# Expert visits as two half tiles of 64 rows: rows stationary, weights moving

## The chip, the cores and the metric

One Trainium2 chip, one core. The metric is the device time in microseconds (us) of one execution; smaller is better. The kernel is written by hand: every engine has its own instruction list, and semaphores order them.

## What is computed

Patch embedding of 32 images (1,184 tokens of 256 numbers), one block of linear attention with a gate and a norm, then a mixture of experts. All data is float32. The part that the change touches, cut from the reference:

```python
logits = x @ gate_weight.T                       # 32 experts in 4 groups
...                                              # 2 groups of 4, then 6 experts per token
tw = tw / (tw.sum(-1, keepdims=True) + 1e-20) * ROUTED_SCALE
eo = silu(x @ w_gate[e]) * (x @ w_up[e]) @ w_down[e]      # 256 -> 128 -> 256
routed = sum over the 6 experts of tw * eo
shared = silu(x @ shared_w_gate) * (x @ shared_w_up) @ shared_w_down
lg = topidx[:, 0] // 2                           # one of 16 anchor experts, 256 -> 64 -> 256
out = routed + shared + 0.1 * anchor(lg)
```

## The kernel before, in words

**Front part.** Blocks of two token tiles (111 tokens each) go through embedding, attention, norm and routing as a hand-written pipeline. When a block is routed, GpSimd (POOL) scatters each token's row (256 numbers and its weights and destinations, `ROW` = 322 words) with an indirect DMA into `rows_d` in DRAM, once for each of its 7 choices: 77 scatters in all (`scatter`). There is one list of rows for each of the 48 experts (32 routed, 16 anchors).

**Visit table.** After the last block is routed, VectorE (DVE) works out a table from the lengths of the lists: for each visit the place of the expert's weights in `W`, the first row, the column of the weight and the place of the sum tile (some 85 small instructions, ending in `cols_ok`). TensorE (PE) turns it into one row (`table_rows`), DVE copies it to `table`, and a second PE product with two DVE steps makes the mask `valid` (`slot_bounds`). The weights of all experts are in SBUF (`W`) by then. While the table is made PE does matmuls that serve nothing (`stay_busy`).

**Visits.** There are `XT` = 112 visits of 128 rows: 25 of anchors, 87 of routed experts. A visit `i` is, in order: SyncE (SP) reads its first row from the table with a register load and issues one DMA of 128 rows into `G` (six buffers, `load_rows`); PE transposes it in two pieces (`turn_rows`, L812); ScalarE (ACT) or DVE copies the transpose to SBUF (`turned_copy`, L985, L1580) and ACT copies the expert's gate and up weights from their place in `W`, which is known only at run time, to a fixed buffer `UPW` (`copy_up`, L981); PE multiplies, weights stationary and rows moving, 4 products of 128x128x128 for a routed expert and 2 for an anchor (`up`, L823); ACT takes silu (L990), DVE multiplies by the up half (`hidden`, L1597); PE multiplies with the down weights, 256 columns (`down`, L838). A float32 product is two PE instructions. PE does up(i), the transposes of i+2, down(i-1), up(i+1).

**Results.** A routed visit on a full tile of one list ("F") is weighted by ACT and sent. A visit on a tile in which rows of two lists meet ("M", "X", and the anchors) is weighted and added by DVE into a tile of sums (`accumulate`, L1589), which is sent when its last visit is in. POOL sends with an indirect DMA of 128 rows into `sums_d` (L483), 66 in all. The tiles of sums lie in `spent` and `ring`, which POOL fills with zeros first (L476, L480).

**End.** When all is sent, SP loads the seven parts of each token back from `sums_d` (L419), DVE adds them to `h`, and SP writes the output.

Of the kernel before, what the change touches and what calls it, by code (L numbers as in the profile page):

```python
# [17 lines left out]
F32 = mybir.dt.float32  # L18
I32 = mybir.dt.int32
# [42 lines left out]
DUMMY_ROW = P + LISTS * LIST_ROWS  # L62
# [7 lines left out]
ROWS_PACKED = -(-TOKENS * TOPK // P)  # L70
LAST_FILLED = TOKENS * TOPK % P
FULL = -(-(TOKENS * TOPK - EXPERTS * (P - 1)) // P)
MIXED = ROWS_PACKED - FULL
EXTRAS = EXPERTS - 1
ANCHOR_PACKED = -(-TOKENS // P)
ANCHOR_TILES = ANCHOR_PACKED + ANCHORS - 1
KINDS = "A" * ANCHOR_TILES + "FFX" * 12 + "XM" * 6 + "XMM" * 13
XT = len(KINDS)
INDEX = [KINDS[:i].count(k) for i, k in enumerate(KINDS)]
TILE_AXIS, EXTRA_AXIS = 1000, 2000  # L80
RING = D + 1
GB = 6
PL = 3 * EXPERTS + ANCHORS


def routed(i):
    return KINDS[i] != "A"


def summed(i):  # L90

    return KINDS[i] != "F"


def sums_before(i):
    return sum(summed(k) for k in range(i))


def copied_by_act(i):
    return KINDS[i] != "F"  # L100


def copies_before(i):
    return sum(copied_by_act(k) == copied_by_act(i) for k in range(i))


def number_of(i):

    return {"A": 0, "F": TILE_AXIS, "M": TILE_AXIS + FULL, "X": EXTRA_AXIS}[KINDS[i]] + INDEX[i]


FIRST_ROUTED = ANCHOR_TILES
EARLY_COLS = 19482
TRI4 = 3 * LISTS
SMALL = TRI4 + 23
PIECES = [[(0, 4), (4, 8), (8, NT)]] * (CHOICES - 1) + [[(0, 4), (4, 7), (7, 9), (9, 10), (10, NT)]]
assert KINDS.count("F") == FULL and KINDS.count("M") == MIXED and KINDS.count("X") == EXTRAS
assert all(KINDS[:i].count("X") >= min(EXTRAS, INDEX[i] + 1) for i in range(XT) if KINDS[i] == "M")
assert FULL * D <= ANCHOR_COLS and XT <= P
# [4 lines left out]
def build(nc, pt, wt, posr, brow, wqkv, wo, wg1, wg2, lnwb, gwt, gbias, sgu, sd, wx,  # L124
          ident_c, cmask_c, turn_c, parity_c, cs_c, before_c, small_c, out):
    with ExitStack() as ctx:
# [56 lines left out]
        def dense(*shape):  # L183
# [5 lines left out]
            if len(shape) == 2:  # L189
# [16 lines left out]
        mixed = spent[:, 0:MIXED * RING]  # L206
        mixed_rows = mixed.bitcast(I32)
# [5 lines left out]
        of_lists = small[:, 0:3 * LISTS].rearrange("p (q l) -> p q l", q=3)  # L213
        iota_a, base0, tri4 = small[:, LISTS:LISTS + ANCHORS], small[:, 2 * LISTS:3 * LISTS], small[:, TRI4:TRI4 + 16]
        pcol, number, of_number, tile_number, spare_row, last_tile, first_w = (small[:, TRI4 + 16 + q:TRI4 + 17 + q]
                                                                                  for q in range(7))
        ring = sb("ring", [P, ANCHOR_PACKED * RING])
        h = sb("h", [P, NT, D])
        ring_rows = ring[:, :].bitcast(I32)
        token_row = sb("token_row", [P, 2, NT], I32)  # L220
        to_rows = sb("to_rows", [P, NT])
        spare = sb("spare", [P, 2])
# [32 lines left out]
        whole = sb("whole", [P, 2 * LISTS], I32)  # L255
        tcol = sb("tcol", [P, 24])
        valid = turn
# [3 lines left out]
        def later(n):  # L261
# [6 lines left out]
        GT = later(2 * D).rearrange("p (u k s) -> p u k s", u=2, k=KC)  # L268
        S = later(2 * P).rearrange("p (u s) -> p u s", u=2)
        H = later(2 * P).rearrange("p (u s) -> p u s", u=2)  # L270
        tabs = e_sb[:, 0:at[0]]
        edges = later(2 * P).rearrange("p (u s) -> p u s", u=2)
        H_anchor = edges
        UPW = sb("UPW", [P, 2, UP_COLS])
        wcol = sb("wcol", [P, XT])
        tok_full = sb("tok_full", [P, FULL], I32)
        Y = W[:, 0:FULL * D].rearrange("p (f d) -> p f d", d=D)
        parts = W[0:TP, 0:CHOICES * NT * D].rearrange("p (c t d) -> p c t d", c=CHOICES, t=NT)

        B = [ctx.enter_context(nc.psum_tensor(f"B{i}", [P, 512], F32)) for i in range(8)]  # L280

        rows_d = nc.dram_tensor("rows_d", [DUMMY_ROW + 2 * P, ROW], F32).ap()
        sums_d = nc.dram_tensor("sums_d", [SPARE_ROW + P, D], F32).ap()
# [22 lines left out]
        g_ld = [sem(f"g_ld{u}") for u in range(GB)]  # L306
        edges_ok, valid_ok, mixed_zero = sem("edges_ok"), sem("valid_ok"), sem("mixed_zero")
        gt_by = {True: sem("gt_by_act"), False: sem("gt_by_dve")}
        T_ps, U_ps, silu_ok, H_ok, upw_ok, D_ps, Y_ok = (
            sem("T_ps"), sem("U_ps"), sem("silu_ok"), sem("H_ok"), sem("upw_ok"), sem("D_ps"), sem("Y_ok"))  # L310
        meta_ok, acc_ok, ring_ok, ids_ok, spared = sem("meta_ok"), sem("acc_ok"), sem("ring_ok"), sem("ids_ok"), sem("spared")
        sent_anchor, sent_full, sent_mixed = sem("sent_anchor"), sem("sent_full"), sem("sent_mixed")
# [4 lines left out]
        def entry(engine, q, i, top):  # L317

            return nc.values_load(table[0:1, q, bass.ds(i, 1)], engines=(engine,), min_val=0, max_val=top,  # L319
                                  skip_runtime_bounds_check_because="the table is computed within these bounds")  # L320
# [28 lines left out]
        def _(sp):  # L349
# [26 lines left out]
            of_list = rows_d[0:LISTS * LIST_ROWS, :].rearrange("(l r) n -> r l n", r=LIST_ROWS)  # L376
            for half in range(2):
                sp.dma_start(of_list[half * P:(half + 1) * P, :, :],
                             padrow[:, :].unsqueeze(1).to_broadcast([P, LISTS, ROW])).then_inc(empty, 16)
            sp.dma_start(W[:, 0:late[0]], wx[:, 0:late[0]]).then_inc(ld["lists"], 16)  # L380

            for half in range(2):
                sp.dma_start(rows_d[DUMMY_ROW + half * P:DUMMY_ROW + (half + 1) * P, :], padrow[:, :]).then_inc(ini_d, 16)
# [17 lines left out]
            sp.wait_ge(ini_d, 16 * 4)  # L401
# [3 lines left out]
            def load_rows(i):  # L405
                if i == FIRST_ROUTED:
                    sp.wait_ge(scat, 16 * NT * TOPK)
                if i >= GB:

                    sp.wait_ge(T_ps, i - GB + 1)  # L410
                    sp.wait_ge(meta_ok, i - GB + 1)
                row = entry(mybir.EngineType.SP, 1, i, DUMMY_ROW + P)
                sp.dma_start(G[:, i % GB, :], rows_d[bass.ds(row, P), :]).then_inc(g_ld[i % GB], 16)
# [6 lines left out]

            for i in range(XT):
                load_rows(i)
                if i == XT - 16:
                    sp.wait_ge(sent_anchor, 16 * ANCHOR_PACKED)
                    sp.wait_ge(sent_full, 16 * FULL)
                    load_part(TOPK)
            sp.wait_ge(D_ps, XT)
            sp.wait_ge(sent_mixed, 16 * MIXED)
# [9 lines left out]
        def _(pool):  # L438
# [10 lines left out]
            pool.memset(ring[:, :], 0.0).then_inc(ring_ok, 1)  # L449
# [25 lines left out]
            pool.wait_ge(hs_ok, NB)  # L475
            pool.memset(spent[:, 0:until_scattered], 0.0).then_inc(mixed_zero, 1)  # L476
            pool.wait_ge(scat_anchor, 16 * NT)
            pool.wait_ge(scat, 16 * NT * TOPK)
            pool.wait_ge(ini_d, 16 * 4)
            pool.memset(spent[:, until_scattered:MIXED * RING], 0.0).then_inc(mixed_zero, 1)  # L480

            def send(rows, src, done):
                pool.indirect_dma_start(sums_d, bass.IndirectOffsetOnAxis(ap=rows, axis=0), src, None).then_inc(done, 16)  # L483

# [1231 lines left out]
```

## Time and profile before

| what | value |
|---|---|
| device time, median of 3 runs | 418.36 us (414.25 to 418.94) |
| profiled execution, span | 412.1 us |
| PE busy | 343.3 us (83%) |
| PE weight load busy | 299.1 us (73%) |
| DVE busy | 278.0 us (67%) |
| ACT busy | 190.0 us (46%) |
| POOL busy | 181.7 us (44%) |
| visit stage, from the first transposes to the first load of parts | 203.1 to 379.95 us |

The span is the time from the first to the last instruction of one profiled execution; a device time of its own is not given for that execution, and the median of the runs is 6.3 us above the span. "Busy" is the time in which an engine had an instruction at work. Times below count from the start of the span.

### The profile page before, as it was taken

The numbers are of one execution on the slowest core, as the hardware profiler recorded it, in microseconds if no ns is written. First come the engines' busy times: TensorE is split into PE (matmuls) and PEld (weight loads), VectorE is DVE, ScalarE is ACT, GpSimd is POOL, SyncE is SP. The second block draws the span as 40 slices with busy tenths as digits, with TensorE's granted clock in tenths as the row PEclk, the third lists the DMA queues.
The fourth block names the chain that finished last, engine by engine and source line by source line (L and its number), as shares of the span: only waits on it lengthen the run. The fifth ranks groups of instructions, "written<-read, shape, count | busy, mean of one in ns | idle before, by whom it ended". The sixth has DMA issues, their size and how long they took to land.

```text
span 412.1 us, 8817 instructions
## 1 busy us (share of the span) xinstructions
PE 343.3 (83%) x2552; PEld 299.1 (73%) x2552; DVE 278.0 (67%) x1171; ACT 190.0 (46%) x471; POOL 181.7 (44%) x159
## 2 busy tenths in 40 slices
PE   5999999999899968773889999999999999994000
PEld 3786978779687857561677789999999999993000
DVE  0466789989798886798357775555565665666675
ACT  1152153441545233400157777777877777771000
POOL 6000000588888768767871374344422344433000
PEclk9999999999999997985989999999999999998555
DMA  7999999986698643694555576555555559531998
GB/s 234 298 335 335 329 341 328 420 320 119 123 337 252 126 96 86 218 387 137 152 162 130 167 214 180 162 158 165 165 145 162 166 155 291 168 113 58 303 303 245
DMA packets 55823, 88.44 MB, mean 215 GB/s; under 512 B 16145, under 2 KB 46521, under 8 KB 55513
## 3 DMA queue, kind: packets, MB, share of 16 engines
q1 hardware_dynamic: 38192, 67.66, 52.9%
q0 software_dynamic: 16720, 19.48, 17.8%
q10 hardware_dynamic: 864, 0.73, 0.6%
q8 instruction: 21, 0.34, 0.3%
q14 instruction: 26, 0.21, 0.2%
HBM read 50.62 MB, written 37.09 MB: 213 GB/s over the span
## 4 chain that ended last, share of the span: by engine, by line
PE 60%; DVE 20%; DMA 8%; issue 3%; ACT 3%; SPq 3%; DVEq 2%; POOLq 0%
PE B L823 20%; PE B L838 10%; PE B L514 6%; PE B L812 5%; DMA W<-sums_d 4%; PE B L549 4%; PE B L632 3%; PE B L598 2%; PE B L618 2%; DVEq L319 2%; DMA e_sb<-rows_d 2%; SPq L419 2%; DVE ring L1589 1%; PE B L656 1%; DMA W<-in_pt 1%
## 5 line engine op out<-in xcount | busy, mean ns | idle before, releaser
L457 POOL DMA_INDIRECT rows_d<-spent,slot x77 | 104.1, 1352 | 97.3 <-issue 90.9
L823 PEld LDWEIGHTS B<-e_sb,UPW 128*128 128x128 f32 x796 | 105.4, 193 | 10.7 <-issue 5.5
L823 PE MATMUL B<-e_sb,UPW 128*128 128x128 f32 x796 | 108.9, 278 | 1.5 <-issue 1.5
L1597 DVE TENSOR_TENSOR e_sb<-e_sb,B 128x128 f32<-128x128 f32 (+1 forms) x112 | 32.3, 288 | 62.2 <-ACT e_sb L990 55.8
L981 ACT COPY UPW<-W 128x512 f32 (+1 forms) x112 | 63.9, 570 | 22.2 <-issue 13.9
L838 PE MATMUL B<-W,e_sb 128*128 x224 | 69.3, 391 | 0.8 <-DVE e_sb L1597 0.8
L483 POOL DMA_INDIRECT sums_d<-spent x32 | 31.1, 972 | 48.7 <-DVE spent L1589 47.9
L812 PE MATMUL B<-ident,e_sb 128*128 128x128 f32 x224 | 43.1, 274 | 1.9 <-DMA e_sb<-rows_d 1.8
L990 ACT ACTIVATE e_sb<-B 128x128 f32<-128x128 f32 (+1 forms) x112 | 30.9, 276 | 22.2 <-PE B L823 20.8
L514 PE MATMUL B<-W 128*111 128x256 f32 (+1 forms) x132 | 34.2, 406 | 4.6 <-DMA W<-in_pt 4.5
L483 POOL DMA_INDIRECT sums_d<-W,tok_full x24 | 23.2, 966 | 30.3 <-ACT W L995 29.7
L838 PEld LDWEIGHTS B<-W,e_sb 128*128 128x128 f32 x224 | 34.0, 192 | 3.5 <-issue 1.7
L985 ACT COPY e_sb<-B 128x256 f32<-128x256 f32 x88 | 32.3, 367 | 4.6 <-PE B L812 4.6
L514 PEld LDWEIGHTS B<-W 128*111 128x111 f32 (+1 forms) x132 | 23.3, 184 | 12.2 <-DMA W<-in_pt 5.3
L1589 DVE SCALAR_TENSOR_TENSOR spent<-B,wcol,spent 128x256 f32<-128x256 f32 (+1 forms) x63 | 30.4, 482 | 1.7 <-DVE spent L1574 0.8
L812 PEld LDWEIGHTS B<-ident,e_sb 128*128 128x128 f32 x224 | 28.5, 144 | 2.3 <-DMA e_sb<-rows_d 2.1
L1626 DVE TENSOR_TENSOR h<-h,W 112x1024 f32<-112x1024 f32 (+3 forms) x23 | 23.2, 1047 | 8.4 <-DMA W<-sums_d 8.4
L1289 DVE TENSOR_TENSOR e_sb<-B,spent 111x444 f32<-111x444 f32 (+1 forms) x44 | 23.6, 597 | 4.1 <-PE B L598 4.1
L1566 DVE TENSOR_TENSOR wcol<-e_sb,turn 128x1 f32<-128x1 f32 x112 | 17.2, 153 | 4.0 <-PE B L812 3.8
L598 PE MATMUL B<-W 32*111 32x222 f32 (+1 forms) x176 | 15.5, 369 | 4.8 <-ACT W L909 4.8
L549 PE MATMUL B<-W 128*128 128x222 f32 (+1 forms) x96 | 18.1, 341 | 0.6 <-ACT W L886 0.6
L606 PE MATMUL B<-spent 128*128 128x256 f32 x70 | 18.6, 414 | 0.0
(250 smaller groups left out, 524.0 us busy)
## 6 DMA issues: line engine op xcount, KB each, us to landing
e_sb<-rows_d SPq DMA_DIRECT2D x112, 161.0 KB, 2.3
rows_d<-spent SPq DMA_DIRECT2D x2, 7728.0 KB, 44.4
W<-in_wx SPq DMA_DIRECT2D x1, 6643.0 KB
W<-sums_d SPq DMA_DIRECT2D x13, 448.0 KB, 9.4
W<-in_wx SPq DMA_DIRECT2D x10, 516.5 KB, 9.5
W<-in_wx SPq DMA_DIRECT2D x1, 4576.0 KB, 18.7
W<-in_pt SPq DMA_DIRECT2D x4, 666.0 KB, 6.9
W<-sums_d SPq DMA_DIRECT2D x7, 336.0 KB, 11.1
```

The source lines that it names most:

```text
L457: pool.indirect_dma_start(rows_d, bass.IndirectOffsetOnAxis(ap=slot[0:n, t, j:j + 1], axis=0), xrow[0:n, t, :], None).then_inc(done, 16)
L483: pool.indirect_dma_start(sums_d, bass.IndirectOffsetOnAxis(ap=rows, axis=0), src, None).then_inc(done, 16)
L514: m = pe.matmul(B[0][0:TILES[t], i * D:(i + 1) * D], patch_view(b)[:, c, at:at + TILES[t]], w_patch[:, c, :], start=c == 0, stop=c == PC - 1)
L549: m = pe.matmul(B[4 + half][:, c * BT:c * BT + n], w_qkv[:, k, lo:lo + P], xnT[:, k, 0:n], start=k == 0, stop=k == KC - 1)
L812: m = pe.transpose(B[i % 2][:, k * P:(k + 1) * P], G[:, i % GB, k * P:(k + 1) * P], ident[:, :])
L823: mm = pe.matmul(B[2 + i % 2][:, m * P:(m + 1) * P], UPW[:, i % 2, at:at + P], GT[:, i % 2, k, :], start=k == 0, stop=k == KC - 1)
L838: pe.matmul(B[6 + i % 2][:, 0:D], hid[:, i % 2, :], weights, start=True, stop=True).then_inc(D_ps, 1)
L981: act.copy(UPW[:, i % 2, 0:n], W[:, bass.ds(e, size)][:, 0:n]).then_inc(upw_ok, 1)
L985: act.copy(GT[:, i % 2, :, :].rearrange("p k s -> p (k s)"), B[i % 2][:, 0:D]).then_inc(gt_by[True], 1)
L990: act.activation(S[0:n, i % 2, :], B[2 + i % 2][0:n, 0:P], ACT.Silu).then_inc(silu_ok, 1)
L1589: dve.scalar_tensor_tensor(sums, B[6 + i % 2][:, 0:D], wcol[:, i:i + 1], sums, ALU.mult, ALU.add).then_inc(acc_ok, 1)
L1597: dve.tensor_tensor(out[0:n, i % 2, :], S[0:n, i % 2, :], ups, ALU.mult).then_inc(H_ok, 1)
```

## The change

The visits get another shape. A visit still has 128 row slots, but as two halves of 64 rows, each from any list: 17 visits of anchors, 71 routed, 88 in all (`VISITS`), taken two at a time in 44 rounds (`ROUNDS`). A list's last half may hold fewer than 64 rows of its own; the slots left over are sent to spare rows of `sums_d`. Every row is in one visit only, so nothing is added up: each visit is sent by itself, 88 sends.

In a round PE transposes four pieces (as before), multiplies with the rows stationary (64 columns of the array for each half, `tile_position=(0, lo)`) and the weights moving (256 columns for routed, 128 for anchors), then goes to the down products of the round before, the transposes of two rounds on, and two transposes of the hidden rows, which the new layout needs. The first half's weights are read where they lie in `W`; the second half's are copied by DVE to `up_w` and `down_w`. DVE picks the row's weight and destination with a comparison (`columns`), and multiplies by the weight in `hidden`. ACT copies the results of both visits at once. SP reads four first rows and issues four DMAs of 64 rows a round, with buffers for three rounds. The table has fewer steps; the lists' area is filled with zeros for 64 rows a list and no longer 256.

```diff
@@ SP
-                row = entry(mybir.EngineType.SP, 1, i, DUMMY_ROW + P)
-                sp.dma_start(G[:, i % GB, :], rows_d[bass.ds(row, P), :]).then_inc(g_ld[i % GB], 16)
+                if r >= GB // 2:
+                    sp.wait_ge(T_ps, r - GB // 2 + 1)
+                    sp.wait_ge(meta_ok, r - GB // 2 + 1)
+                rows = [entries(mybir.EngineType.SP, 2 + half, r, LAST_ROW - HALF) for half in range(2)]
+                for j in range(2):
+                    for half in range(2):
+                        sp.dma_start(G[half * HALF:(half + 1) * HALF, (2 * r + j) % GB, :],
+                                     rows_d[bass.ds(rows[half][j], HALF), :]).then_inc(g_ld[r % (GB // 2)], 16)
@@ POOL
-            pool.memset(spent[:, 0:until_scattered], 0.0).then_inc(mixed_zero, 1)
...
+            for v in range(VISITS):
+                if v % 2 == 0:
+                    pool.wait_ge(Y_ok, v // 2 + 1)
+                    pool.wait_ge(meta_ok, v // 2 + 1)
...
+                pool.indirect_dma_start(sums_d, bass.IndirectOffsetOnAxis(ap=row_to[:, v:v + 1], axis=0), results(v),
+                                        None).then_inc(done, 16)
@@ PE
-            stay_busy(12, 3, w_sgu)
+            stay_busy(7, 3, w_sgu)
             table_rows()
+            spread_columns()
             shared_down(3)
-            slot_bounds()
@@
+            def up(r, own_weights):
+                pe.wait_ge(GT_ok, r + 1)
+                pe.wait_ge(up_staged, r + 1)
+                for j in range(2):
...
+                    for k in range(KC):
+                        for half, w in enumerate((first, second)):
+                            lo = half * HALF
+                            m = pe.matmul(B[2 + r % 2][lo:lo + HALF, j * D:j * D + n], GT[:, r % 2, j, k, lo:lo + HALF],
+                                          w[:, k * n:(k + 1) * n], start=k == 0, stop=k == KC - 1, tile_position=(0, lo))
+                m.then_inc(U_ps, 1)
+            def turn_hidden(r):
+                pe.wait_ge(H_ok, r + 1)
...
+                for j in range(2):
+                    m = pe.transpose(B[4 + r % 2][:, j * P:(j + 1) * P], H[:, j, :], ident[:, :])
+                m.then_inc(HT_ps, 1)
+            def down(r, own_weights):
...
+                    for half, w in enumerate((first, second)):
+                        lo = half * HALF
+                        m = pe.matmul(B[6 + r % 2][lo:lo + HALF, j * D:(j + 1) * D], HT[:, j, lo:lo + HALF], w,
+                                      start=True, stop=True, tile_position=(0, lo))
...
+                up(r, own_weights)
+                if r >= 1:
+                    down(r - 1, before_own)
+                if r + 2 < ROUNDS:
+                    turn_rows(r + 2)
+                turn_hidden(r)
@@ ACT
+            for r in range(ROUNDS):
+                hidden_silu(r)
+                if r >= 1:
+                    result_copy(r - 1)
+                hidden_copy(r)
+                if r + 2 < ROUNDS:
+                    turned_copy(r + 2)
@@ DVE
+            def stage_up(r):
+                places = weights_of(mybir.EngineType.DVE, 1, r)
...
+                if r >= 2:
+                    dve.wait_ge(U_ps, r - 1)
+                for j in range(2):
+                    hidden, size = widths(2 * r + j)
+                    n = KC * 2 * hidden
+                    m = dve.tensor_copy(up_w[:, (2 * r + j) % 4, 0:n], W[:, bass.ds(places[j], size)][:, 0:n])
+                m.then_inc(up_staged, 1)
+            def stage_down(r, places):
...
+                    m = dve.tensor_copy(down_w[:, (2 * r + j) % 4, :], W[:, bass.ds(places[j], size)][:, n:n + D])
+                m.then_inc(down_staged, 1)
+            def columns(r):
+                dve.wait_ge(T_ps, r + 1)
...
+                    m = dve.scalar_tensor_tensor(own[:, j, :, :], iota_to.unsqueeze(1).to_broadcast([P, 2, TO_ROW]),
+                                                 expert_col[:, v:v + 1], both, ALU.is_equal, ALU.mult)
+                step(m)
+                dve.reduce_sum(wcol[:, r % 2 * 2:r % 2 * 2 + 2], own[:, :, 0, :], axis=AX.X).then_inc(weight_ok, 1)
+                step(dve.reduce_sum(to_sum[:, :], own[:, :, 1, :], axis=AX.X))
+                dve.tensor_tensor(row_to[:, 2 * r:2 * r + 2], to_sum[:, :], spare_to[:, 2 * r:2 * r + 2], ALU.add).then_inc(meta_ok, 1)
...
+            for r in range(ROUNDS):
+                hidden(r)
+                if r + 2 < ROUNDS:
+                    places.append(stage_up(r + 2))
+                if r + 1 < ROUNDS:
+                    stage_down(r + 1, places[r + 1])
+                    columns(r + 1)
```

## Rows read from the trace of the kernel before

**Rows 1.** Stretches of time: from:to, length, busy time of each engine, PE clock.

```profile
178.80:192.60 13.80, 5.49 (x23) 4.39 (x22) 12.81 (x85) 0.00 (x0) 11.05 (x9) 0.75 0.80 272
...
240.50:373.10 132.60, 132.60 (x1031) 128.20 (x1031) 77.39 (x346) 102.18 (x259) 54.42 (x58) 1.00 0.58 169
380.00:412.10 32.10, 0.00 (x0) 0.00 (x0) 19.96 (x20) 0.00 (x0) 0.00 (x0) 0.50 0.92 275
```

**Rows 2.** Timeline of one routed visit: start, length, engine, line, idle and releaser.

```profile
302.33 1.05 PE L823 MATMUL B<-e_sb,UPW 128*128 128x128 f32 x8
...
303.23 0.38 PE L812 MATMUL B<-ident,e_sb 128*128 128x128 f32 x2
...
303.43 0.28 ACT L990 ACTIVATE e_sb<-B 128x128 f32<-128x128 f32 x1 [0.27 <-PE B L823]
303.44 0.60 PE L838 MATMUL B<-W,e_sb 128*128 x2
...
303.73 0.29 DVE L1597 TENSOR_TENSOR e_sb<-e_sb,B 128x128 f32<-128x128 f32 x1 [0.56 <-ACT e_sb L990]
```

**Rows 3.** Timeline of PE, attention of tile 0: products in four column tiles.

```profile
36.45 0.98 PE L618 MATMUL B<-e_sb,W 111*32 111x111 f32 x32
37.35 0.60 PE L539 MATMUL B<-ident,W 111*128 111x111 f32 x4
37.88 0.98 PE L618 MATMUL B<-e_sb,W 111*32 111x111 f32 x32
```

**Rows 4.** Groups by form, routed stage: count, busy us, mean ns, idle before.

```profile
L981 ACT COPY UPW<-W 128x512 f32 x86 | 53.2, 618 | 15.9 <-issue 9.8
L985 ACT COPY e_sb<-B 128x256 f32<-128x256 f32 x63 | 23.1, 366 | 0.0
L1589 DVE SCALAR_TENSOR_TENSOR spent<-B,wcol,spent 128x256 f32 x30 | 14.5, 485 | 1.2 <-DVE spent L1574 0.8
```

**Rows 5.** Groups by form of DVE, whole span: wide operations from SBUF.

```profile
L1626 DVE TENSOR_TENSOR h<-h,W 112x512 f32<-112x512 f32 x1 | 0.7, 685 | 0.0
L1525 DVE TENSOR_SCALAR e_sb<-ident,tcol 128x128 f32<-128x128 f32 x1 | 0.3, 275 | 0.0
```

**Rows 6.** Timeline, 187.3 to 188.8 us: DVE beside a scatter of POOL.

```profile
187.38 1.35 POOL L457 DMA_INDIRECT rows_d<-spent,slot  x1 [0.30 <-issue]
187.38 0.24 DVE L1497 TENSOR_SCALAR e_sb<-e_sb,tcol 128x32 f32<-128x32 f32 x1
...
188.09 0.61 DVE L1501 COPY e_sb<-e_sb 128x16 f32<-128x16 f32 x1
```

**Rows 7.** SP's row loads (L413) and register loads (L319, by stretch): ns min/median/max.

```profile
L413 SPq DMA_DIRECT2D e_sb<-rows_d x112: 332/333/808, 196.8 to 363.4; - x112
...
DMA to landing us min/median/max: 2.2/2.3/6.2
...
L319 SPq TENSOR_LOAD <-scratch x8: 285/1160/1447, 195.3 to 206.6; - x8
...
L319 SPq TENSOR_LOAD <-scratch x102: 262/268/712, 212.5 to 363.0; - x102
```

**Rows 8.** POOL's last scatters and its routed sends: ns min/median/max.

```profile
L457 POOL DMA_INDIRECT rows_d<-spent,slot x19: 1348/1349/1354, 175.1 to 207.2; - x19
...
DMA to landing us min/median/max: 4.9/5.7/10.5
...
L483 POOL DMA_INDIRECT sums_d<-spent x30: 963/964/967, 301.8 to 372.8; - x30
```

**Rows 9.** Timeline: the table's first step, what waits for it, scatters landed, sends, end.

```profile
178.83 0.19 DVE L1441 SCALAR_TENSOR_TENSOR e_sb<-base,small 128x32 f32<-128x32 f32 x1
...
192.59 1.87 PE L711 MATMUL B<-ident,tcol 128*1 128x128 f32 x8 [8.31 <-DVE tcol L1524]
...
214.50 3.26 POOL L480 MEMSET spent<- 128x3791 f32 x1 [2.10 <-issue]
...
379.95 11.10 SPq L419 DMA_DIRECT2D W<-sums_d  x19
```

More of the change, by code:

```diff
@@ L1422, in tab @@
                 return v
-            starts, ends, total, of_tile, mine = tab(PL), tab(PL), tab(E), tab(E), tab(PL)
-            facts = tab(4 * PL).rearrange("p (q l) -> p q l", q=4)
-            offset, many, shifted, slot_tile = (facts[:, q, :] for q in range(4))
-            held, begin, end, full, lead, behind = tab(LISTS), tab(LISTS), tab(LISTS), tab(E), tab(LISTS), tab(LISTS)
-            new, away, some, rounded, over, span, own = (tab(LISTS), tab(LISTS), tab(LISTS), tab(E), tab(E), tab(ANCHORS),
-                                                         tab(LISTS))
@@ L1447, in _ @@
-            step(dve.tensor_copy(full, whole[:, 0:E]))
-            dve.scalar_tensor_tensor(held[:, LR], full, -float(P), total, ALU.mult, ALU.add)
-            step(dve.tensor_tensor_scan(ends[:, R], ones_of, full, float(TILE_AXIS), ALU.mult, ALU.add))
-            dve.tensor_copy(first_c, ends[:, E - 1:E])
-            dve.tensor_scalar(some, held, 0.0, None, ALU.is_gt)
-            dve.tensor_tensor(starts[:, R], ends[:, R], full, ALU.subtract)
-            step(dve.tensor_tensor_scan(end[:, LR], ones_of, held[:, LR], 0.0, ALU.mult, ALU.add))
@@ L1467, in _ @@
-            step(dve.tensor_copy(lead[:, 1:LISTS], whole[:, 0:LISTS - 1]))
-            dve.tensor_tensor(new[:, 1:LISTS], lead[:, 1:LISTS], lead[:, 0:LISTS - 1], ALU.is_equal)
-            dve.scalar_tensor_tensor(away, lead, -float(P), begin, ALU.mult, ALU.add)
-            dve.scalar_tensor_tensor(over, of_tile, -float(P), rounded, ALU.mult, ALU.add)
-            dve.tensor_tensor(span, span, lead[:, LA], ALU.subtract)
-            dve.tensor_scalar(starts[:, M], lead[:, LR], first_c, None, ALU.add)
@@ L1473, in _ @@
-            step(dve.tensor_scalar(ends[:, M], of_tile, first_c, None, ALU.add))
-            dve.scalar_tensor_tensor(own[:, LR], new[:, LR], -1.0, away[:, LR], ALU.add, ALU.mult)
-            dve.scalar_tensor_tensor(own[:, LA], new[:, LA], -1.0, away[:, LA], ALU.add, ALU.mult)
-            dve.scalar_tensor_tensor(over, over, 0.0, some[:, LR], ALU.is_gt, ALU.mult)
-            step(dve.tensor_tensor(span, span, some[:, LA], ALU.mult))
-            dve.tensor_tensor_scan(shifted[:, M], new[:, LR], own[:, LR], 0.0, ALU.mult, ALU.add)
```

567 lines of the change are left out of this document (230 added, 337 removed).

## The prediction

> **What bounds the kernel now.** I read the stretches first [rows 1]. From 240.5 to 373.1 us, the 86 routed visits between the first and the last up product, PE is busy for all 132.6 us at full clock; ACT (102.2), DVE (77.4) and POOL (54.4) are not. 132.6/86 gives 1.54 us a visit. One visit's timeline [rows 2] shows how PE fills it: 8 up instructions from 302.33 to 303.23, so 0.112 us each for 128 columns, two transposes at 0.11 (303.23 to 303.44), and two down instructions of 256 columns in 0.44 until the next up at 303.88. Ahead of it are the 25 anchor visits, and ahead of those the table: DVE works alone from 178.8 to 192.6 (85 instructions, PE clock 0.75) [rows 1], and PE's `table_rows` waits 8.3 us for it [rows 9]. Behind the visits the parts come back from 379.95 on, 32.1 us at 275 GB/s on which the change has no hand [rows 1, 9]. So the question is what a round costs, and when the routed rounds can begin.
>
> **PE's work in a round.** Transposes: 4 of rows and 2 of hidden rows, 6 x 0.11 = 0.66 us. Up: 8 products, 16 instructions of 256 columns at 0.22. Down: 4 products, 8 instructions at 0.22. One behind the other that is 3.46 + 1.73 us; in pairs, half. Whether column tiles run beside each other the trace does show: attention's L618 uses four tiles of 32 columns with a full depth of 111 rows and a different moving operand in each, and 32 instructions take 0.98 us with the last one's tail [rows 3]. At 111/128 x 0.112 = 0.097 each they would take 3.1 us alone; the last begins some 0.72 us in, so four ran at a time. I take pairs: 1.73 + 0.865. The change back to a full array is in the same rows: the last L618 ends at 37.43 and, with 0.26 us of its own length, began at about 37.16; L539 begins at 37.35, 0.09 us late against the step of 0.097. The other way L618 begins at 37.88 and L539's fourth at about 37.69, 0.09 late again. L539's three steps take 0.60 - 0.26 = 0.34 and not 0.29, 0.05 more. Two changes a round: 0.26. PE's round is 0.66 + 1.73 + 0.87 + 0.26 = 3.52 us for a routed pair, against 2 x 1.54 = 3.09 before: more for each visit, but 71 visits and not 87. 35.5 x 3.52 = 125 us against 87 x 1.54 = 134. An anchor round is 0.66 + 0.9 + 0.87 + 0.26 = 2.7 us.
>
> The Trainium skill, "TensorEngine Tiling (Array Packing)", Key Properties, says that changing the tiling mode drains TensorE, a rule that speaks against mixing full transposes and half tiles in each round. By the rows it costs 0.26 us a round, 11 us over 44 rounds; free of it the round would be 3.26 us.
>
> **Does PE get its data in time?** I lay one round out from the start of its up products (T = 0). Last up instruction begins at 1.5, and ends as modelled 0.38 later, ACT's silu follows 0.04 behind (303.43, [rows 2]): 1.93. Silu of 256 columns: 0.28 for 128 and 0.1 more, to 2.32. DVE's two products with the weight, 0.2 + 0.35 (0.485 for 256 columns from PSUM [rows 4]; 1.05 ns a column): 2.85. PE does down(r-1) and the row transposes until 3.2, so `turn_hidden` doesn't wait. ACT: silu 0.38, results 0.58, hidden rows 0.37, turned rows 0.58 (0.366 for 256 columns, 0.83 ns for each more, [rows 4]), 1.9 us in all; ACT is not the bound, and loses `copy_up`, 53.2 us.
> DVE then does what is new. A register load, 0.3. Two copies of 512 columns and two of 256, SBUF to SBUF. No such copy is in the trace. Above: an operation of two sources, 0.685 for 512 [rows 5]. Below: one source, 0.24 for 32 columns and 0.275 for 128 [rows 5, 6], 0.4 ns a column, so 0.45 for 512. I take the second, the nearer kind; in steps (without the tail of each) about 0.32 + 0.32 + 0.19 + 0.19, with addresses 1.2 us; by the first it would be 1.9. `columns` is five small operations with two waits, 0.9. DVE's round: 0.5 + 0.3 + 1.2 + 0.9 = 2.9 us (3.6 by the dear price), ending at T = 5.0.
> SP: two register loads (0.27 each in this stretch, [rows 7]; if each register needs its own, four), four DMAs at 0.333 + 0.2 for addresses and sequencing: 2.85 us, or 3.4. The last lands 2.3 us after its issue: 4.8 us from `meta_ok` to rows. The load of round r waits for `columns(r-3)`, done at T = 5.0 of slot r-4, and `turn_rows(r)` is at T = 2.75 of slot r-2: 2P + 2.75 >= 5.0 + 4.8, P >= 3.53 us. Before, this chain had six visits of room; now it is as long as PE's round, and everything that makes DVE later adds half of itself to P.
> What makes DVE later is POOL. At 188.09 a copy of 16 columns takes 0.61 us and ends with POOL's scatter that began at 187.38 (188.73); a like operation at the scatter's start, 187.38, takes 0.24 [rows 6]. A scatter holds such DVE operations in its second half. Before, the visits had none from SBUF to SBUF; now four a round meet two sends of 0.96 us [rows 8]. `result_copy` ends at T = 3.4, so the first send's second half (3.9 to 4.4) falls on the down copies: I take 0.4 us, P = (5.4 + 4.8 - 2.75)/2 = 3.73, and **3.75** as the forecast. POOL itself needs 2 x 1.3 = 2.6 us, under P: 88 sends and not 66 cost nothing while that holds.
>
> **The table.** About 27 operations with 10 waits take the place of 85: 0.2 + 0.3 + 0.35 + 0.35 + 0.4 + 0.6 + 0.65 + 0.35 for the dependent steps up to `cols_ok`, with a hold by POOL about 4 us, where 13.8 were. The table is ready some 10 us sooner. What is late next: SP's first rows, from about 187 us (the last anchor scatter has 17 behind it at 1.35 + 0.30, so it begins at 207.2 - 28 = 179, and lands 5.7 to 10.5 us after its issue, [rows 6, 8]). POOL still scatters until 208.6, and there SP's register loads take 1.16 us [rows 7]: 4.6 us a round. Rounds 0 to 4 are issued by 209.5, then one in 2.85. All scatters have landed at 214.5, when POOL's second fill starts [rows 9], so round 8, the first with routed rows, may be loaded. The chain of buffers puts `turn_rows(8)` at 224.5 and slot 8, the first routed one, at **227.5**, where before the first routed up product ran at 240.5. With quick anchor slots it would be 223; with four register loads 235. The fills with zeros before the visits and DVE's sums go, hidden already; the smaller zero fill of the lists frees writes in the front part, for which no engine but POOL waits, and POOL's last scatter is set by the last block's slots: nothing.
>
> **The end.** From the last slot's start: `turn_hidden` done at 3.1 + 0.3, copy 0.37, down 0.9 + 0.2, result 0.58, two sends 2.3, landing 1.5: 9.3 us, against 6.85 before (373.1 to 379.95).
>
> **Sum**, in the span of the profiled execution: 227.5 + 35 x 3.75 + 9.3 + 32.15 = 400.2 us, against 412.1. Gains: 13 us ahead of the routed rounds, 1.4 in them, less 2.5 at the end. The median of the runs lies 6.3 us above the span: **406.5 us**.
>
> **Rivals.**
> 1. *PE sets the round* (P = 3.52, quick anchor slots): the port hold misses DVE's copies. 223 + 123.2 + 9.3 + 32.15 + 6.3 = 394 us. For it: ACT, DVE and SP are each under 3 us. Against: the load chain is 3.53 without any delay.
> 2. *DVE is held for whole sends*, or its copies cost the dear price: columns end 1.2 us later (P >= 4.1), DVE's own round is 4.2 to 4.4. P = 4.3: 227.5 + 150.5 + 9.3 + 32.15 + 6.3 = 425.8, slower than before. It decides from P = (418.36 - 6.3 - 32.15 - 9.3 - 227.5)/35 = 4.09. The Trainium skill, "SBUF — State Buffer", Who interferes with whom, has this mechanism: a VectorE copy that uses both port pairs and a GpSimd operation lock each other out for the whole instruction. Rows 6 agree in kind, but the operation at the scatter's start ran free, so the hold is less than whole there.
> 3. *The half tiles don't overlap*: the sequence per product is pass, pass, other half, and fp32 with 64 columns is not in the trace. Then P = 3.46 + 1.73 + 0.66 + 0.26 = 6.1, anchor slots 4.4: 236 + 213.5 + 12 + 32.15 + 6.3 = 500 us. Against it, rows 3, made of the same two-pass products.
>
> **Chances.** Forecast (P 3.6 to 4.0, 401 to 415 us) 0.46; rival 1 0.2; rival 2 (415 to 436) 0.27; rival 3 0.07. A change of 2% is about what a measurement of this kernel tells from none: 410.0 and 426.7 us. Faster: 0.2 and 0.34 of the forecast's 0.46, 0.54. Within: 0.12 and 0.18 of rival 2, 0.30. Slower: 0.16. The range for 8 in 10: 392 (rival 1 with P 3.5) to 432 (P 4.3 with slot 8 at 234); rival 3 is left out.
>
> **What the profile after would show.** Right: up instructions of 256 columns beginning in pairs, about 1.75 us from the first up to the first down of a round; a period of 3.75 us; DVE's first copy 0.4 to 0.5 us, stage_down copies stretched beside a send; PE's idle time put down to the row DMAs or to DVE's columns; `table_rows` 10 us earlier; first routed up near 227.5. Wrong: PE steps of 0.22 with no pairs (rival 3); a period over 4.1 with DVE busy above 90% (rival 2); the tail longer than 32 us. My sum would also fail if PE's clock fell in the gaps of the anchor rounds and stayed low, which no row of the visits before shows.

## The result, and the profile after

The changed kernel takes 452.57 us (median of 4 runs, 451.65 to 455.45) beside 418.65 us of the kernel before (4 runs, 414.25 to 420.54): a ratio of 1.085, interval 1.078 to 1.092. It is slower, outside the range of the prediction. Medians here and below are of all executions, ratios and their 95% intervals of those in the faster of the two states in which a kernel runs.

Stretches of the kernel after, as in [rows 1]: from:to, length, busy time of PE, PEld, DVE, ACT and POOL, PE's granted clock, share and rate of the DMA engines.

```profile
181.30:185.70 4.40, 3.32 (x12) 2.40 (x10) 4.10 (x19) 0.00 (x0) 3.48 (x3) 0.83 1.04 386
...
211.30:245.80 34.50, 25.70 (x234) 19.15 (x234) 17.34 (x81) 12.58 (x30) 12.05 (x13) 0.82 0.44 127
245.80:403.50 157.70, 131.01 (x1046) 83.03 (x1046) 94.15 (x388) 64.12 (x142) 71.64 (x71) 0.97 0.47 140
414.60:450.40 35.80, 0.00 (x0) 0.00 (x0) 20.40 (x20) 0.00 (x0) 0.00 (x0) 0.50 0.94 247
```

The first row is the table, 4.4 us where [rows 1] have 13.8. The second is the eight anchor rounds, the third the routed ones from the first to the last up product: 157.7 us for 35 periods, 4.51 us each, with PE busy for 131.0 of them, where 35 x 3.52 = 123.2 were foreseen. Before, PE was busy for all of its 132.6 us. So the larger part of the loss in this stretch is not work of PE, but 27 us in which it stands. Who it stands for is in the page, part 5 (busy, mean ns, idle before, releaser):

```profile
L806 PE MATMUL B<-W,e_sb 128*64 x352 | 84.6, 388 | 5.7 <-issue 2.6
L806 PE MATMUL B<-up_w,e_sb 128*64 128x256 f32 (+1 forms) x352 | 84.8, 388 | 0.0
L790 PE MATMUL B<-ident,e_sb 128*128 128x128 f32 x176 | 30.8, 301 | 43.9 <-DMA e_sb<-rows_d 43.8
```

Over the whole kernel `turn_rows` (L790) waits 43.8 us for row DMAs. In the routed stretch alone it is 21.8 of the 27 us; 4.1 more are waits ahead of the up products (L806). The timeline of PE in a round that nothing disturbs:

```profile
336.32 0.42 PE L806 MATMUL B<-W,e_sb 128*64 x1
336.32 0.43 PE L806 MATMUL B<-up_w,e_sb 128*64 128x256 f32 x1
336.58 0.38 PE L806 MATMUL B<-W,e_sb 128*64 x1
336.59 0.38 PE L806 MATMUL B<-up_w,e_sb 128*64 128x256 f32 x1
...
338.09 0.38 PE L832 MATMUL B<-W,HT 128*64 x1
...
339.06 0.66 PE L790 MATMUL B<-ident,e_sb 128*128 128x128 f32 x4
339.55 0.38 PE L816 MATMUL B<-ident,H 128*128 128x128 f32 x2
340.19 0.42 PE L806 MATMUL B<-W,e_sb 128*64 x1 [0.25 <-DVE up_w L1478]
```

The two halves begin 0.01 us apart, then nothing for 0.21 us: full pairs. From the first up to the first down product it is 1.77 us (predicted: about 1.75), and from there to the transposes 0.97. The round is 3.87 us, and 3.87 is the least that any routed round shows; I had 3.52.

A disturbed round, as the chain of waits gives it piece by piece (start, length, what):

```profile
296.89 0.53 SPq L303
...
297.45 0.48 SPq L303
...
298.10 0.47 SPq L406
...
298.75 0.47 SPq L406
...
299.41 0.47 SPq L406
...
300.06 4.33 DMA e_sb<-rows_d
...
304.43 0.66 PE B L790 x4
305.09 0.22 PE B L816 x2
305.31 0.12 issue
305.43 3.50 PE B L806 x16
```

Two register loads of two values, 0.53 and 0.48 us ([rows 7] have 0.268 for one value); four issues of 64 rows at 0.47 and 0.18 between them ([rows 7]: 0.333 for 128 rows); then 4.33 us from the last issue until PE can use the rows (2.6 to 2.7 in most rounds where PE waits for them and they come quickly, 2.45 in one). PE has stood since 302.3, and when it goes on its up products take 3.50 us and not 1.77: over 305.4 to 308.9 the granted clock is 0.54, so nearly all of it at the lower of TensorE's two levels (1.2 and not 2.4 GHz), where 301.9 to 304.4, in which PE stood for 2.1 us, still showed 1.00. This late row cost twice.

The front, line by line of SP's queue (ns min/median/max), the loads of rounds 0 to 2 while GpSimd scatters:

```profile
L303 SPq TENSOR_LOAD <-scratch x6: 555/1133/2639, 190.2 to 207.0; - x6
...
L406 SPq DMA_DIRECT2D e_sb<-rows_d x12: 468/827/1812, 191.8 to 210.9; - x12
```

### The profile page after: what moved, and what is told of

It is laid out like the page before. It is cut to its first block, busy times and chain, and to the rows that moved or that the text cites. A ratio compares the mean times of both kernels' runs of the same rounds, so it can differ in the third digit from the quotient of the medians.

```text
span 450.4 us, 8512 instructions
## 1 busy us (share of the span) xinstructions
PE 335.6 (75%) x2622; PEld 246.9 (55%) x2622; DVE 281.3 (62%) x1141; ACT 142.9 (32%) x312; POOL 199.6 (44%) x178
## 4 chain that ended last, share of the span: by engine, by line
PE 27%; DVE 17%; issue 16%; DMA 14%; SPq 11%; POOL 10%; ACT 3%; DVEq 1%; POOLq 0%
POOL sums_d L474 10%; SPq L406 5%; DMA e_sb<-rows_d 5%; DMA W<-sums_d 5%; PE B L490 5%; PE B L806 4%; SPq L303 3%; PE B L525 3%; DMA rows_d<-spent,slot 2%; PE B L608 2%; PE B L574 2%; DMA W<-in_wg 2%; SPq L413 1%; PE B L594 1%; PE B L790 1%
## 5 line engine op out<-in xcount | busy, mean ns | idle before, releaser
L474 POOL DMA_INDIRECT sums_d<-spent,turn x56 | 57.6, 1029 | 72.6 <-ACT spent L1002 63.8
L806 PE MATMUL B<-W,e_sb 128*64 x352 | 84.6, 388 | 5.7 <-issue 2.6
L806 PE MATMUL B<-up_w,e_sb 128*64 128x256 f32 (+1 forms) x352 | 84.8, 388 | 0.0
L806 PEld LDWEIGHTS B<-W,e_sb 128*64 128x64 f32 x352 | 46.8, 147 | 31.4 <-issue 18.0
L790 PE MATMUL B<-ident,e_sb 128*128 128x128 f32 x176 | 30.8, 301 | 43.9 <-DMA e_sb<-rows_d 43.8
L790 PEld LDWEIGHTS B<-ident,e_sb 128*128 128x128 f32 x176 | 19.7, 148 | 62.2 <-DMA e_sb<-rows_d 46.7
L474 POOL DMA_INDIRECT sums_d<-W,turn x32 | 32.8, 1025 | 38.9 <-ACT W L1002 34.0
L832 PE MATMUL B<-W,HT 128*64 x176 | 46.5, 388 | 0.5 <-ACT HT L995 0.5
L806 PEld LDWEIGHTS B<-up_w,e_sb 128*64 128x64 f32 x352 | 46.9, 147 | 0.0
L832 PE MATMUL B<-down_w,HT 128*64 128x256 f32 x176 | 46.5, 388 | 0.0
L1478 DVE COPY up_w<-W 128x512 f32 (+1 forms) x88 | 31.8, 403 | 10.1 <-issue 8.7
L980 ACT COPY e_sb<-B 128x512 f32<-128x512 f32 x44 | 26.0, 592 | 20.3 <-PE B L790 20.3
## 6 DMA issues: line engine op xcount, KB each, us to landing
e_sb<-rows_d SPq DMA_DIRECT2D x176, 80.5 KB
```

The lines of the kernel that those rows point to most:

```text
L790: m = pe.transpose(B[r % 2][:, j * D + k * P:j * D + (k + 1) * P], G[:, (2 * r + j) % GB, k * P:(k + 1) * P], ident[:, :])
L806: m = pe.matmul(B[2 + r % 2][lo:lo + HALF, j * D:j * D + n], GT[:, r % 2, j, k, lo:lo + HALF], w[:, k * n:(k + 1) * n], start=k == 0, stop ...
L832: m = pe.matmul(B[6 + r % 2][lo:lo + HALF, j * D:(j + 1) * D], HT[:, j, lo:lo + HALF], w, start=True, stop=True, tile_position=(0, lo))
L980: act.copy(GT[:, r % 2, :, :, :].rearrange("p j k s -> p (j k s)"), B[r % 2][:, 0:2 * D]).then_inc(GT_ok, 1)
L1478: m = dve.tensor_copy(up_w[:, (2 * r + j) % 4, 0:n], W[:, bass.ds(places[j], size)][:, 0:n])
```

## The experiments

Theory A: the row supply closes on itself over two rounds (DVE's columns done, SP's wait, two register loads, four issues, landing, turning), and it is longer than the 2P of the forecast, 7.5 us. What each rival is stands with each expectation. Each run has its own run of the kernel before beside it on the same chip. "Slot n" is the start of round n's up products; P is the mean period from slot 8 to slot 43. In the kernel after: slot 0 at 211.4, slot 8 at 245.8, slot 43 at 403.5, P 4.51.

**1. DVE's columns a round sooner.** `columns(1)` ahead of the loop, and in it:
```
             if r + 1 < ROUNDS:
                 stage_down(r + 1, places[r + 1])
-                columns(r + 1)
+            if r + 2 < ROUNDS:
+                columns(r + 2)
```


> The changed kernel with DVE's columns taken one round sooner (columns(r+2) at the end of DVE's round r, where it was columns(r+1)), so that the wait of SP's row loads on meta_ok ends a round sooner. Theory A (the chain columns, SP's two register loads and four DMA issues, landing, row transposes sets the period of a round, 4.51 us on average): the chain gets a round of room, the period falls to the 3.87 us that undisturbed rounds have, 35 x 0.6 us less, and some 4 us in the anchor rounds: 425 to 432 us. Theory B (PE's register load behind the wait for the hidden rows sets it): no change, 448 to 455. Theory C (PE's clock falls by itself, whatever the loads do): half of A or less, above 440.


Measured: 433.9 us (1.025, 1.016 to 1.034, of before), slot 8 at 242.5, P 4.12, median round 3.87. It takes 19 us off, without a change on PE; the time is 2 us above the range of theory A.

**2. SP's register loads ahead of its waits.**
```
         def load_rows(r):
+            rows = [entries(SP, 2 + half, r, ...) for half in range(2)]
             if r == FIRST_ROUTED:
...
-            rows = [entries(SP, 2 + half, r, ...) for half in range(2)]
```


> The changed kernel with SP's two register loads of a round (0.48 us each) ahead of its waits on T_ps and meta_ok instead of behind them. Theory A: the chain is 1.0 us shorter, (5.46 + 4.9 - 2.75)/2 = 3.8 us, under the 3.87 of undisturbed rounds, so about the same as the run before: 427 to 436 us. Theory B: no change, 448 to 455. If only the number of instructions on SP mattered and not what waits for them, there would be no change either, since none is taken away.


Measured: 440.1 us (1.047, 1.038 to 1.056), slot 8 at 242.7, P 4.24, median 3.87; the time is 4 us above the range. Two edits on two engines, each on the chain, are worth 19 and 12 us, and in both most rounds stop at 3.87. A fourth round of row buffers, which would also give the chain room, was not tried.

**3. PE's register loads ahead of its wait.** PE loads the weights' places of round r+1 before `turn_hidden(r)` and not behind it.


> The changed kernel with PE's register load for the next round's weights (0.54 us) ahead of the wait for the hidden rows and not behind it. Theory A: the row chain stays, so the time moves little, 446 to 453 us, and rounds that no row load disturbs fall from 3.87 to about 3.55 us. Theory B: 35 x 0.3 us and more, 435 to 441.


Measured: 450.7 us (1.066, 1.055 to 1.076), P 4.46, but undisturbed rounds now take 3.55. The floor of 3.87 was PE's own register load behind the wait for H_ok; by itself taking it away gives little, since the chain sets most rounds.

**4. All three.**


> All three edits together. Theory A: the row chain is off the path, and so is PE's register load; next is SP itself, which needs 2 x 0.5 + 4 x 0.65 = 3.6 to 3.75 us a round, so the period is 3.7 us: 452.6 - 35 x 0.8 - 5 = 419 to 424 us. If DVE's copies and POOL's sends hold each other (rival 2 of the prediction) the period stays above 4.1 and the time above 433.


Measured: 430.8 us (1.029, 1.022 to 1.035), P 3.92, most rounds 3.54 or 3.55. PE's round is thus what the prediction worked out, 3.52. The time misses theory A's range (419 to 424): rounds 39 and 40 alone took 8.8 and 5.3 us, and without them the mean is 3.74, since about one round in three still waits for rows.

**5. The anchor part's load last.** `load_part(TOPK)`, with its waits for the sends, moved from `r == ROUNDS - 4` to behind the loop.


> The kernel with all three edits, and the load of the anchor part moved behind the last load of rows in the sync engine's queue. Theory A (rounds 39 and 40, of 8.8 and 5.3 us where the others have 3.55, waited for rows whose issue stood behind the wait and the three issues of that part): every routed round is under 4.2 us, the mean over the routed rounds falls from 3.92 to about 3.6, slot 43 starts about 7 us sooner, time 422 to 426 us. Rival (the two slow rounds come from the sums' or weights' traffic at that place): they stay, 430 us.


Measured: 427.2 us (1.027, 1.017 to 1.036), P 3.83, those two rounds 3.55. The cause of the two slow rounds is right. Slot 43 comes 3.6 us sooner, half of what I expected, since rounds of 4 to 5 us remained, and the time is above the expected range. In the ratios (1.029 and 1.027) the gain is not clear of noise; it is read from the rounds.

**6. The kernel before, each load of 128 rows as two of 64.**
```
-    sp.dma_start(G[:, i % GB, :], rows_d[bass.ds(row, P), :]).then_inc(...)
+    for half in range(2):
+        sp.dma_start(G[half * 64:(half + 1) * 64, i % GB, :],
+                     rows_d[bass.ds(row + half * 64, 64), :]).then_inc(...)
```


> The kernel before, with each load of 128 rows issued as two loads of 64 rows; nothing else is changed. Measures by itself what the halves cost the sync engine. Theory A (an issue for 64 rows costs it 0.47 us, as in the changed kernel, not the 0.33 us of an issue for 128): a visit then costs the sync engine 0.27 + 2 x 0.65 = 1.6 us against a visit's period of about 1.5, so the time rises by 2 to 12 us, and the issues show 0.45 to 0.48 us each. Rival (the 0.47 us comes from what else the changed kernel does in that time, and an issue costs about 0.33): the visit costs it 0.27 + 2 x 0.5 = 1.3 us, hidden, time within 2 us of before.


Measured: 456.3 us (1.090, 1.080 to 1.099). The price is theory A's, the effect much more than I gave it:

```profile
L414 SPq DMA_DIRECT2D e_sb<-rows_d x208: 468/469/2107, 212.5 to 399.4; - x104
```

The same bytes in the same order, 0.469 us an issue and not 0.333, and SP's step for a visit is 1.68 us without any stall, against PE's 1.54. With the stalled ones among them (0.50 mean issue, 0.31 mean register load, and waits) the mean step from visit 10 on is 1.81, where the kernel before has 1.53. A loss as large as that of the change appears in a kernel that has none of its half tiles. It is the same price, met in another way: here SP's work for a visit is longer than PE's, in the changed kernel SP's work lies in a chain that closes over two rounds.

**7. Two issues more per round**, small and to a place nobody reads, behind the four row loads of the changed kernel. An earlier run was to double the two register loads; the doubled loads left no instruction in the program (88 register loads of SP in both traces), so that run was the changed kernel once more (449.7 us, 1.078, 1.067 to 1.089) and tested nothing:


> The changed kernel with the sync engine's two register loads of each round done twice (about 1.0 us more per round, nothing else). Theory A (the chain wait, register loads, four issues, landing, turn, copy, column work closes on itself over two rounds): half of it shows in each round, so the routed mean goes from 4.5 to 4.9 to 5.1 us, and with the anchor rounds the time to 470 to 482 us. Rival (the slow rounds come from the memory traffic, not from this queue): under 458 us.


The one that can't vanish:


> The changed kernel, and the sync engine issues two small transfers more in each round (64 rows of 512 bytes to a place that nobody reads), right behind the four row loads. The run with the doubled register loads held the same instructions as the changed kernel, so it told nothing; this one can't vanish. Theory A: if each costs 0.5 to 0.65 us, the queue has 1.0 to 1.3 us more a round, but an issue behind the last row load delays only the next wait, which comes late anyway where the queue idles at it (1.5 us a round at a mean of 4.5), so the added cost is hidden up to that: the routed mean rises by 0 to 0.3 us, time 455 to 470 us with the front, where the queue is full. Rival (the queue is not the limit in any stage): within 2 us of 452.


Measured: 491.1 us (1.177, 1.167 to 1.188), P 5.41. Above the range I gave, because I took SP's idle time for 1.5 us a round; it works 3.7 of 4.5. The chain of waits of this run, from 300 to 311 us, is SP and nothing else: laps of 5.26 us with a slow register load in them, and 5.03 without, and no wait. The two transfers also load the memory, but no landing stands in the chain. The shares there:

```profile
by line: SPq L408 40.1%; SPq L420 33.7%; SPq L305 19.4%; issue 12.3%; SPq L404 0.3%
```

**8. GpSimd's last scatters held** until PE has turned the rows of round 0, or of round 1 (`pool.wait_ge(T_ps, 1)`, or 2, ahead of the last loop of scatters), on top of run 5.


> As the one with the anchor part last, and GpSimd holds its last run of scatters (about 18 of them, 1.65 us apart, 186 to 212 us) until TensorE has turned the first round's rows. Theory C (the scatters' descriptors and traffic slow the sync engine's register loads to 0.8 to 2.6 us and the landing of the first rows to 9 us; without them the first rows land at 194 to 197 us): slot 0 starts at 200 to 204 us instead of 212, scatters end about 220 to 224, slot 8 starts at 234 to 237 instead of 244, time 414 to 419 us. Rival D (slot 0 is set by something else in the front, or the held scatters delay the routed rows by as much): slot 8 stays at 243 or later, time 423 us or more.

> As the run with the scatters held, but until the second round's rows are turned. Theory C: slot 0 at 198 to 202 us with no wait for the second rows, scatters end 224 to 228, so the first routed rows land at 233 to 236 and slot 8 starts at 235 to 240; time 414 to 421 us. Rival D: slot 8 at 243 or later.


Measured: 428.3 us (1.025, 1.017 to 1.033) and 428.3 (1.023, 1.014 to 1.032); slot 0 at 202.0 and 202.2 and not 213.3, but slot 8 at 245.6 and 247.4. So rival D's slot 8, and both times miss theory C's range (414 to 419, and 414 to 421). Yet the mechanism of theory C stands in the second run, SP's register loads and row issues before the scatters and during them (they start at 202.6 us; the first two lines count to 205, the others from there to 230):

```profile
L303 SPq TENSOR_LOAD <-scratch x8: 467/470/682, 191.4 to 203.6; - x8
...
L406 SPq DMA_DIRECT2D e_sb<-rows_d x14: 468/469/590, 192.7 to 205.0; - x14
```
```profile
L303 SPq TENSOR_LOAD <-scratch x6: 717/1420/2346, 206.8 to 223.9; - x6
...
L406 SPq DMA_DIRECT2D e_sb<-rows_d x15: 468/714/1877, 205.0 to 229.8; - x15
```

The scatters slow the queue wherever they are. Held, the 17 of them, 1.65 us apart until 230.5, meet the loads of later rounds: the periods of rounds 2 to 4 are 8.2, 7.5 and 8.2 us. The loss is moved, not saved.

**9. Round 0's up products ahead of the turning of round 1's rows**, on PE, ACT and DVE, on top of run 5.


> The kernel with the three edits and the anchor part last (427 us), with TensorE, ScalarE and VectorE doing round 0 ahead of the turning of round 1's rows. Theory C (the front is set by how fast the sync engine gets the rows of the anchor rounds issued while GpSimd scatters): slot 0 starts 3 to 6 us sooner, at 207 to 210, but slot 8 stays within 2 us of 243.7, time 425 to 428 us. Rival (the order at the start costs it): slot 8 at 240 or sooner, time 420 to 423 us.


Measured: 427.1 us (419.6 to 431.6, 4 runs; before 418.0), slot 0 at 205.5, slot 8 at 243.5: theory C by slot 8, though slot 0 came sooner than it said. The order at the start costs nothing by the slots; the times, of which one lies 7 us under the other three, decide nothing.

**10. The kernel before once more**, for the tail.


> The kernel before, unchanged, for its profile beside those of this chip. It tells what the slower tail is: from the first load of parts to the end before took 32.2 us, the changed kernel 35.9, and the kernel before with rows in two halves 35.8 with its sums unchanged. Theory T1 (the tail's reads are slower by the kernels' own doing): 32 to 33 us again. Theory T2 (it differs from chip to chip or from hour to hour): 35 us or more here.


Measured: 421.1 us, (one run), from the first load of parts to the end 32.7 us (386.5 to 419.2). T1, but only in part: the run that equals the changed kernel had 33.7 where the changed kernel had 35.9, and the kernel before with its rows in halves, which has its sums unchanged, 35.9. What makes the reading of the sums slower by 1 to 5 us stays open; their size and place do not explain it.

**11. The rows by two queues.** ScalarE issues the lower half tiles, the sync engine the upper, on top of run 5:
```
+    def load_lower(r):
+        ...                       # the same waits as load_rows
+        rows = entries(Activation, 3, r, LAST_ROW - HALF)
+        for j in range(2):
+            act.dma_start(G[HALF:P, (2 * r + j) % GB, :],
+                          rows_d[bass.ds(rows[j], HALF), :]).then_inc(g_ld[...], 16)
     for r in range(ROUNDS):
         hidden_silu(r)
         ... result_copy(r - 1)
+        load_lower(r + 4)
```


> The kernel with the three edits and the anchor part last (427 us), and ScalarE issues the two loads of the lower half tiles (one register load 0.47 us and two issues, about 1.8 us of its 3.55 us per round beside 1.7 of own work), the sync engine only those of the upper. Theory A and C (row supply by one queue is what still makes some rounds 4 to 5 us and the anchor rounds slow): slot 8 starts at 232 to 238 us instead of 243.7, routed mean 3.6 to 3.7 instead of 3.83, time 413 to 420 us. Rival E (ScalarE is full with it, or its copies wait behind register loads and issues): routed mean 3.9 or more, time 428 us or more.


Measured: 418.7 us (1.001, 0.996 to 1.006), slot 8 at 240.0, P 3.79. The same bytes, the same number of DMAs, and 8 us less than with one queue. Slot 8 gained 3.7 us, where 6 to 12 were expected, and P is above the 3.6 to 3.7 of theory A.

With run 9's order added:


> As the run with the lower rows by ScalarE (418.7 us), with round 0 done ahead of the turning of round 1's rows. Theory C: slot 8 stays within 2 us of 240, time 416 to 420 us. Rival (the order at the start costs it): slot 8 at 237 or sooner, time 413 to 416 us.


Measured: 420.3 us (1.011, 1.005 to 1.016), slot 8 at 240.1. Again the order gained nothing.

**12. Three and one.** As the run before it (the order of run 9 included), but in the routed rounds SP issues three of the four, ACT one.


> As the one before it, but in the routed rounds the sync engine issues three of the four row loads and ScalarE one (0.27 + 0.65 us instead of 1.8 us a round). If ScalarE's load is what keeps most rounds of the split version at 3.6 to 3.8 us and not 3.55, the routed mean falls from 3.79 to 3.6 to 3.7 and the time to 410 to 415 us, below the kernel before. Rival: the sync engine's queue delays some rows again, routed mean 3.8, time 417 us or more.


Measured: **410.0 us (0.975, 0.964 to 0.985)**, faster than the kernel before: all four runs (405.3 to 412.3) lie under the lowest of the 13 of the kernel before beside them (412.96). Whether it is faster by 2% is not settled. Slot 8 at 239.7, P 3.53. Its routed stretch, as in [rows 1]:

```profile
239.70:363.30 123.60, 123.34 (x1048) 78.92 (x1047) 94.02 (x386) 64.08 (x141) 68.70 (x70) 1.00 0.60 176
```

35 rounds of 3.53 us, PE busy for 123.3 of 123.6 us at full clock, 9 us less than the 86 visits of before.

## Why the prediction was wrong

The sum was off by 50 us of span, in four terms (predicted, measured):

| term | predicted | kernel after | off |
|---|---|---|---|
| slot 8 | 227.5 | 245.8 | 18.3 |
| 35 periods | 131.2 (3.75) | 157.7 (4.51) | 26.5 |
| last slot to first load of parts | 9.3 | 11.1 | 1.8 |
| the parts | 32.15 | 35.8 | 3.7 |

- **PE's work, right.** Pairs, 0.216 us a step, a round of 3.55 where nothing else holds it (runs 4 and 12) against 3.52 worked out; that leaves 0.30 for the two changes of tiling, 0.26 by the rows. Rival 3 falls. What the sum has no term for, though it has one for DVE's and SP's, is PE's register load behind the wait for the hidden rows: 0.32 us a round, 3.87 in place of 3.55 (run 3).
- **The step that failed: "SP: two register loads, four DMAs at 0.333 + 0.2: 2.85 us", and the 4.8 us from `meta_ok` to rows built on it.** I kept the prices of a one-value load and a 128-row issue. They are 0.5 each and 0.65 with sequencing: 3.7 us of SP's time a round. (The terms as written add up to 2.67, not 2.85.) From the end of SP's wait to the last issue it is 3.2 us, and 2.7 more until PE can use the rows, where nothing slows them: 5.9 us. Columns were done at 5.2 to 5.5, 5.46 at the most in rounds whose hidden rows were in time, not at 5.0; the prediction's own terms behind the 2.85 of the hidden rows (0.3, 1.2, 0.9) give 5.25. With these, by the prediction's own formula, P >= (5.46 + 5.9 - 2.75)/2 = 4.3. The form of the chain was right, and so was the remark that it has lost its room: from round 10 on, SP's first register load begins within 0.12 us of the end of DVE's columns in 26 of 34 rounds. Its length decided. What lies between 4.3 and 4.51 has two candidates in the round shown, a slow landing (4.3 us) and PE at its lower clock behind the wait; no run tells their shares apart.
- **Break-even was P = 4.09** by the prediction. With its one size at 4.8 the chain fell below it, with 5.9 above. I priced the dear end of DVE's copies, and no dear end of SP's issues: the size of a DMA was changed, so its old row was a bound on one side only.
- **The hold by GpSimd (rival 2's mechanism): it exists, but the copies do not fall where I put them.** Of the 66 `stage_down` copies from 250 to 400 us, 63 lie wholly within a send, end 0.3 us or more before it does, and take 0.285 us in the mean, as outside it. One would have ended in the send's last part. It took 0.478 us, until 0.09 behind the send's end. The timeline of the usual round and of that one:

```profile
340.03 0.98 POOL L474 DMA_INDIRECT sums_d<-W,turn  x1 [2.39 <-ACT W L1002]
340.09 0.49 DVE L1489 COPY down_w<-W 128x256 f32 x2
```
```profile
277.44 1.14 POOL L474 DMA_INDIRECT sums_d<-spent,turn  x1 [1.60 <-ACT spent L1002]
277.99 0.68 DVE L1489 COPY down_w<-W 128x256 f32 x2
```

  So the send's end holds a copy, as [rows 6] had it. But the send begins at T = 3.7 and not 3.4, beside the copies, and they are done before its second half. The 0.4 us of delay that I took for it was there in one such copy of 66, with 0.2 us (run 1 has nine such copies in its routed rounds, of 0.48 us each), and the copies cost what the cheap price said: 0.427 for 512 columns (0.45), 0.34 in steps. The Trainium skill, "SBUF — State Buffer", Who interferes with whom, has a copy in a two-port mode and a GpSimd operation shut each other out for the whole instruction. These rows agree in kind only: a copy that is done 0.3 us before the send's end goes free beside it, and only the one that reaches its last part is held. Rival 2's time (425.8) and sign came nearer than the forecast, by another cause.
- **Slot 8.** The table came in 4.4 us as predicted (4), and its products at 185.7, 6.9 us sooner than [rows 9]; the first 2.5 us went before it, since the last block's slots came later. Then all was lost again. Rounds 0 to 4 were to be issued by 209.5; three were, by 211.9: a round costs SP 7.2 us there (190.2 to 211.9) and not 4.6, with register loads at 1.13 (median; up to 2.64) and issues at 0.83 (up to 1.81). [rows 7] had shown the slow register loads, and I carried those; that issues slow as well I did not ask, though 0.808 stands in the same rows as their longest. Runs 8 and 9 show that neither the start of slot 0 nor its order matters, run 11 that a second queue gains 4 us. Some 12 us against 227.5 stay in the best version, mostly in rounds 0 and 1 (8.0 and 7.0 us), where the register loads of every engine are slow; no run took the scatters away, so it is not shown that these 12 us can be had.
- **The end.** 11.1 and 35.8 for 9.3 and 32.15. In the first, the last two sends begin at 410.8 and not at 409.1, behind two of the round before that took 1.27 and 1.70 us (the median is 0.98); why they did is open. So is the second, see run 10.
- **"If PE's clock fell in the gaps"** was named as what would break the sum. It did fall, in routed rounds too (0.54 behind the wait of 2.1 us shown above, 0.97 over the stretch), but behind the waits for rows: in run 12, with the rows in time, the routed stretch has 1.00.

The Trainium skill, "DMA: Bandwidth & Descriptors", Issuing engines are not separate DMA queues, says that issuing from several engines saves only the sequencer's time to start a DMA, which is usually small beside the transfer. Here the trace has 0.65 us of SP for each 80.5 KB, four times in 3.55 us; that time was the bound, and sharing it out between two engines gave 17 us (run 5 to run 12, in which the order of run 9, which alone gained nothing in the slots, is also changed).

## What to carry to other kernels

When a change splits a transfer, price the queue that issues it anew: so many issues and register values a round against the round's own length, from the dearest row there is. Where a chain returns over a few buffers, write its whole length, engine by engine, and move off it what waits for nothing (register loads ahead of waits, address work a round early); the engine that sets the pace can be one that the table of busy times does not list at all, as the sync engine here. And hold a bound on each new cost on both sides, above all on those that look too small to matter.

## What the runs showed of the hardware

- A DMA of 64 rows with a register address costs the sync engine 0.468 us to issue, one of 128 rows of the same width 0.333; the halved load is dearer twice over (run 6). ScalarE's issue of 64 rows shows 0.49.
- A register load of two values takes 0.47 to 0.48 us, of one 0.27.
- While GpSimd scatters to DRAM, register loads of two values take 0.56 to 3.0 us (0.47 to 0.68 on the sync engine with the scatters held, run 8), and not on the sync engine alone; in run 12, from 191 to 212 us (ns min/median/max):

```profile
L303 SPq TENSOR_LOAD <-scratch x6: 1297/1728/2985, 191.0 to 212.4; - x6
L303 ACTq TENSOR_LOAD <-scratch x5: 1267/1582/2983, 191.0 to 212.3; - x5
L303 DVEq TENSOR_LOAD <-scratch x3: 1265/1358/2226, 190.8 to 209.7; - x3
```

- Single-precision products of 64 columns of stationary data in two column tiles, each with its own 256 moving columns, run as pairs: 0.216 us a pair, in the same time as one alone of 256 at full width before (0.22).
- A VectorE copy from SBUF to SBUF that would end in the last part of a GpSimd indirect DMA instruction ends 0.09 us behind it instead: 0.48 us for 0.28 beside a send of 0.97 to 1.14, and in the front a copy of 0.73 for 0.29 beside a scatter of 1.35.
